# Edge weights multiplied into the low one-hot blocks by VectorE's comparison instead of by ScalarE, and source numbers split in floating point

## What is computed

```python
# GAT, twice (4 heads of 32)
h = (x @ W).reshape(N, H, C)
e = leaky_relu(alpha_s[src] + alpha_d[dst], 0.2)
e_exp = exp(e - segment_max(e, dst)[dst])
out = segment_sum(h[src] * (e_exp / segment_sum(e_exp, dst)[dst]), dst) + bias
...
# the layer behind them
feat_neigh = segment_sum(edge_val[:, None] * feat_in[edge_col], edge_row)
```

## Time and profile before

| | us |
|---|---|
| median of 3 runs | 12189.33 (12188.68 to 12192.55) |
| the profiled execution | 12168.16 |
| its span, first to last instruction | 12166.3 |
| first GAT pass, from the first gather to the last addition | 417 to 2829 |
| second GAT pass | 2953 to 5650 |

### The profile page before, as it was taken

The page is one execution under the profiler, slowest core; times in us unless marked ns, Lnnn a source line. Parts: engine busy times, 40 slices in busy tenths (PEclk is TensorE's granted clock), DMA queues, the critical chain, the costliest instruction groups (busy, mean ns, idle before and its releaser), DMA issues. The chain is left out here.

```text
span 12166.3 us, 91441 instructions
## 1 busy us (share of the span) xinstructions
PE 3704.8 (30%) x14114; PEld 2564.3 (21%) x14213; DVE 6446.5 (53%) x10684; ACT 2415.0 (20%) x6031; POOL 7481.0 (61%) x7840
## 2 busy tenths in 40 slices
PE   2212233332224555555200000003311111113987
PEld 2212222322113333333200000001211111112433
DVE  6445666664545665563655666665332222223877
ACT  1112333331212233221100000000000000001876
POOL 4676777774767766552576777772276777774023
PEclk7556666665557777778655555556655555556999
DMA  2255444443375665555247444442137333334866
GB/s 59 68 76 92 101 107 108 114 109 58 89 102 150 167 163 160 151 156 144 75 111 103 112 112 112 112 112 35 40 103 92 104 104 107 104 107 122 280 243 214
DMA packets 928552, 1422.94 MB, mean 117 GB/s; under 512 B 191108, under 2 KB 723306, under 8 KB 927992
## 3 DMA queue, kind: packets, MB, share of 16 engines
q0 software_dynamic: 277904, 662.94, 26.4%
q10 hardware_dynamic: 549664, 498.96, 14.4%
q1 hardware_dynamic: 100680, 257.93, 6.3%
HBM read 1064.18 MB, written 355.03 MB: 117 GB/s over the span
## 5 line engine op out<-in xcount | busy, mean ns | idle before, releaser
L818 POOL DMA_INDIRECT ring<-gat_table,index x3640 | 3470.8, 954 | 1536.9 <-issue 1054.2
L818 POOL DMA_INDIRECT ring<-b_table,index x1820 | 1730.2, 951 | 671.0 <-issue 526.0
L818 POOL DMA_INDIRECT ring<-kv_table,index x1820 | 1722.8, 947 | 594.6 <-issue 526.1
L961 PE MATMUL pairs<-hot_lo,hot_hi 128*128 128x128 f32 x6272 | 1173.9, 373 | 1845.9 <-PEq L959 1845.9
L961 PEld LDWEIGHTS pairs<-hot_lo,hot_hi 128*128 128x128 f32 x6272 | 1142.3, 286 | 1922.0 <-issue 1922.0
L993 ACT ACTIVATE hot_lo<-hot_lo,wt 128x128 f32<-128x128 f32 x3136 | 949.4, 387 | 1895.4 <-ACTq L991 1881.5
L1911 DVE TENSOR_TENSOR tb<-bt,att 128x1792 f32 x130 | 263.2, 2025 | 1661.7 <-DVEq L106 1661.7
L1143 DVE TENSOR_TENSOR first<-ring,first 128x924 f32<-128x924 f32 x260 | 292.5, 1125 | 1495.6 <-DVEq L106 1495.6
L1933 PE MATMUL bt<-ident,ring 128*128 128x128 f32 x1820 | 417.2, 421 | 1932.0 <-PEq L106 1932.0
L2066 ACT ACTIVATE r<-kept_ring,coef 128x448 f32<-128x448 f32 x1040 | 763.8, 758 | 184.9 <-ACTq L106 161.0
L713 PE MATMUL tp<-ident,stage 128*128 128x128 f32 x196 | 49.0, 427 | 2444.7 <-DVEq L700 2410.5
(11 more groups left out here) (414 smaller groups left out, 7926.4 us busy)
## 6 DMA issues: line engine op xcount, KB each, us to landing
kept_ring<-kept SPq DMA_DIRECT2D x260, 896.0 KB, 4.6
dense_weights<-dstage ACTq DMA_DIRECT2D x392, 512.0 KB
layer_out<-dense_weights ACTq DMA_DIRECT2D x98, 1568.0 KB, 14.8
kept<-tb ACTq DMA_DIRECT2D x132, 896.0 KB, 3.8
ring<-gat_table,index POOLq DMA_INDIRECT x3640
ring<-kv_table,index POOLq DMA_INDIRECT x1820
ring<-b_table,index POOLq DMA_INDIRECT x1820
col<-turned ACTq DMA_DIRECT2D x400, 32.0 KB
```

Source lines behind the costliest of these rows:

```text
L818: pool.indirect_dma_start(self.ring[:, r * UG + i, :], None, self.table, bass.IndirectOffsetOnAxis(self.index[:, half, at:at + 1], 0)).the ...
L961: mm = pe.matmul(self.ps[:, b, i * P:(i + 1) * P], self.hot_hi[:, u, 4 * b + i, :], self.hot_lo[:, u, 4 * b + i, :], start=False, stop=Fal ...
```

## The change

The constants and the preparation of columns change so that every column already carries the offset of its half: in `build_slots`, L470, the dummy value gets 8192 added for the lower partitions' half. The integers, the weights' copy and the semaphores `marked` go. VectorE divides the source number by 128 and rounds to a whole number by adding and subtracting 3 x 2^22, which gives the upper digit, and gets the lower one by subtraction. The low blocks are made one pair at a time by an instruction that compares the ramp with the lower digit and multiplies by the weight, both read as one value a partition. VectorE itself tells TensorE by `built`, after each quad, and frees the column only behind the phase's last block, since the weights are read from it. ScalarE keeps the fetch.

```diff
+WHOLE = float(3 << 22)
...
-                    c.go(dve.tensor_scalar(half[part, w, 0, part], ok[part, :], float(DUMMY), None, ALU.add))
+                    c.go(dve.tensor_scalar(half[part, w, 0, part], ok[part, :], float(DUMMY + q * PITCH), None, ALU.add))
...
-                c.go(dve.tensor_copy(self.wt[:, u, :], self.col[:, u, 1, part]))
-                c(dve.tensor_copy(self.num[:, 0, :], self.col[:, u, 0, part]))
-                dve.sem_inc(self.col_free[u], 1)
-                c(dve.tensor_single_scalar(self.num[:, 1, :], self.num[:, 0, :], 7, ALU.arith_shift_right))
-                c(dve.tensor_single_scalar(self.num[:, 0, :], self.num[:, 0, :], P - 1, ALU.bitwise_and))
-                c.go(dve.tensor_copy(self.lo[:, :], self.num[:, 0, :]))
-                c(dve.tensor_scalar(self.hi[:, :], self.num[:, 1, :], k.upper[:, 0:1], None, ALU.add))
-                c.reset()
+                source = self.col[:, u, 0, part]
+                c(dve.tensor_scalar(self.hi[:, :], source, 1.0 / P, 0.5 * (P - 1) / P, ALU.mult, ALU.subtract))
+                c(dve.tensor_scalar(self.hi[:, :], self.hi[:, :], WHOLE, WHOLE, ALU.add, ALU.subtract))
+                c(dve.scalar_tensor_tensor(self.lo[:, :], self.hi[:, :], float(-P), source, ALU.mult, ALU.add))
                 shape = [P, 4, P]
                 for b in range(QUADS):
                     four = slice(4 * b, 4 * b + 4)
-                    ramp = k.ramp[:, :].unsqueeze(1).broadcast_to(shape)
-                    dve.tensor_tensor(self.hot_hi[:, u, four, :], self.hi[:, four].unsqueeze(2).broadcast_to(shape),
-                                      ramp, ALU.is_equal)
-                    dve.tensor_tensor(self.hot_lo[:, u, four, :], self.lo[:, four].unsqueeze(2).broadcast_to(shape),
-                                      ramp, ALU.is_equal).then_inc(self.marked[b], 1)
+                    c.go(dve.tensor_tensor(self.hot_hi[:, u, four, :], self.hi[:, four].unsqueeze(2).broadcast_to(shape),
+                                           k.ramp[:, :].unsqueeze(1).broadcast_to(shape), ALU.is_equal))
+                    for i in range(4 * b, 4 * b + 4):
+                        w = at + i
+                        last = c.go(dve.tensor_scalar(self.hot_lo[:, u, i, :], k.ramp[:, :], self.lo[:, i:i + 1],
+                                                      self.col[:, u, 1, w:w + 1], ALU.is_equal, ALU.mult))
+                    c.until(last)
+                    dve.sem_inc(self.built[b], 1)
+                dve.sem_inc(self.col_free[u], 1)
+                c.reset()
...
-            for b in range(QUADS):
-                act.wait_ge(self.marked[b], 1)
-                act.sem_inc(self.marked[b], -1)
-                for j in range(4 * b, 4 * b + 4):
-                    last = act.activation(self.hot_lo[:, u, j, :], self.hot_lo[:, u, j, :], ACT.Copy,
-                                          scale=self.wt[:, u, j:j + 1])
-                last.then_inc(self.built[b], 1)
```

More of the change, by code:

```diff
@@ L890, in __init__ @@
         self.col = s.sb("col", [P, 2, 2, CH])
-        self.num = s.sb("num", [P, 2, PP], I32)
-        self.lo, self.hi, self.wt = s.sb("lo", [P, PP]), s.sb("hi", [P, PP]), s.sb("wt", [P, 2, PP])
+        self.lo, self.hi = s.sb("lo", [P, PP]), s.sb("hi", [P, PP])
         self.hot_hi, self.hot_lo = s.sb("hot_hi", [P, 2, PP, P]), s.sb("hot_lo", [P, 2, PP, P])
@@ L896, in __init__ @@
         self.ps = s.ps("pairs", [P, QUADS, 512])
-        self.marked, self.built, self.bank_free = ([k.sem(f"{x}{b}") for b in range(QUADS)] for x in (
-            "marked", "built", "bank_free"))
+        self.built, self.bank_free = ([k.sem(f"{x}{b}") for b in range(QUADS)] for x in ("built", "bank_free"))
         self.used = [k.sem(f"pairs_used{u}") for u in range(2)]
```

## The result

The kernel after took 11897.19 us (median of 4 runs, 11890.97 to 11906.11), the kernel before 12189.01 on the same chip: a ratio of 0.9762, interval 0.9745 to 0.9779. It is 292 us faster; the forecast was 11915. The profiled execution of after took 11906.11 us.

The account below looks back on a forecast made before the run. POOL's gathers bound long bands, ScalarE's late exponent the short ones. Pass two 245 plus pass one 40 less 10 for collisions gives 275: 12168 - 275 = 11893, and 21 more for the runs' median, 11915 us; range 11850 to 12090.

Parts of the forecast that it names:

- What bounds the kernel: POOL's gathers set the long bands; in short bands VectorE waits for ScalarE's late exponent, 698.3 us from 3525.
- the 325 put down as the most that POOL could give back: POOL's waits for ring space in two stretches of the passes, 27.2 and 297.8 us, as the gain's upper limit.
- The tile: Two-unit tile, second pass: quads 1.87 us, phase 8.7, exponent D + 20.5, multiply D + 21.3 (D its start), 35.7 in all.
- the 0.7 for stretched tensor_scalars: Two-unit tile: 0.7 us added for collisions, one tensor_scalar in nine as long as 522 ns against 341.
- Where the gain falls: Pass two from 3525 ends 245 us earlier, pass one from 1971 40 us; stages after 5650 are untouched.
- The 10 us for collisions: Both passes: more gathers beside blocks, up to 7 a phase instead of 5, at 10 to 80 ns each, cost 10 us.
- Rival 1: VectorE becomes the bound: quads near 2.3 us, tiles 39, pass two saves 150, pass one loses 30, 12070 us; chance 14%.
- Rival 2: Each of 7 gathers a phase waits x us longer: passes change -25+686x and -295+686x; 12320 at x=0.33; chance 7%.
- the 1.02 us in the earlier trace: POOL's DMA instruction beside seven two-operand tensor_scalars, against a median of 0.94: the 0.08 argued against rival 2.
- the stop as 0.15 us of cost: VectorE waits for each quad's last low block before marking it, counted as 0.15 us within the quad's 1.87.
- Rival 3: TensorE's clock might not rise with products spread along the builds: TensorE 42.5 us a tile, total 12130; chance 5%.
- Rival 4: The change does nothing because the exponent is late for another reason: 12189 us; chance 4%.

Follow-up runs that it names:

- Runs 1: Kernel before with only the floating-point split of the source numbers, ScalarE still multiplying by the weights: 12199.0 us, 1.0004 of before.
- run 2: Kernel before with the edge weights not multiplied in at all, so ScalarE's scaling pass is gone: 11867.87 us, 0.9729 of before.
- run 3: Kernel after with every low block computed twice, the second time into a tile nobody reads: 12369.51 us, 1.0145 of before.
- run 4: Kernel after without VectorE's stop behind the first three quads of a phase; the quad's last instruction marks it: 11976.55 us, 0.9821 of before.
- run 5: As run 4, with an added 160-column VectorE instruction between quads that reads ramp twice: 12108.92 us, 0.9957 of before.
- run 10: As run 4, with an added 128-column compare-and-multiply between quads that reads only ramp from SBUF besides scalar pointers: 12117.18 us, 0.9963 of before.
- run 6: As run 5, but the added instruction between quads has 40 columns instead of 160: 12045.45 us, 0.9904 of before.
- 7, two wide: Kernel after with a quad's low blocks made by two wide instructions, compare then multiply, stop kept: 11972.67 us, 0.9845 of before.
- 8, hi in PSUM: Kernel after with the tile hi (16 block numbers of a chunk) in PSUM instead of SBUF: 11863.43 us, 0.9751 of before.
- run 9: As run 4, without the stops between quads, but with the block numbers hi in PSUM: 11832.17 us, 0.9726 of before.
- 11, exponents first: Kernel after with ScalarE's exponents of a tile ahead of its first-phase stores and second-phase fetches and copies: 11942.67 us, 0.9816 of before.

## Why the prediction was right, point by point

*What bounds the kernel.* Right. Runs 1 and 2 separate the two halves of the change in the kernel before: the split does nothing, and taking ScalarE's pass away gives 325 us. That this is also the 325 put down as the most that POOL could give back is chance. In all attention gathers POOL's waits for ring space fell from 482.5 to 209.5 us in run 2 and to 213.8 in after; in after another 28 us were won behind the last gather of the passes (from 54.8 and 65.6 us to the pass's last finish down to 34.2 and 58.5), a term that the sentence on the 325 leaves out.

*The tile.* The 1.87 us of a quad, 8.7 of a phase (8.75), exponent at D + 20.5 (20.6), multiply at D + 21.3 (21.3) are as worked out. The compare-and-multiply form takes as long as the multiply-and-add that stood in the earlier trace rows; taking the same shape and operands as the nearest row was the right choice. The two-unit tiles came to 34.4 to 35.3 us, forecast 35.7: the 0.7 for stretched tensor_scalars was one term too many. Its 28 gathers alone take POOL 34.9 us (28 x (0.947 + 0.30)), so here the tile's length does not tell which of the two engines sets it; the waits of both are short.

*Where the gain falls.* Pass one ended 47.5 us earlier (2830.6 to 2783.1, forecast 40). Pass two, from its first gather to its last finish, took 251 less (forecast 245). At the next stage's first gather it is 297 in all (5998.2 to 5701.4), against 285 less 10. Two sums of the forecast don't come out of their terms: 3525 + 669 + 22 + 7 is 4223, not 4231, and 5650 less 5403 is 247, not 245. With them mended the forecast would have been some 10 us nearer. The 10 us for collisions did not come: the attention gathers were busy 3475.2 us, 3470.8 before. The profiled pair differs by 262 us only, since the stages behind, which the change doesn't touch, took 35 us longer in the profiled run of after. Gathers took 3 ns more there at the median, 0.947 us against 0.944 in the earlier trace rows; that is a third of it at most, and the rest is not explained. The medians differ by 292.

*Rival 1, VectorE the bound.* Not at this length of quad, but run 3 shows how near it was: with 1.03 us more a quad the short tiles get longer by all of it.

*Rival 2, the gathers held off.* For this kernel it did not happen, and the reason I gave, the 1.02 us in the earlier trace rows, was of the wrong kind. I looked for the hold beside the tensor_scalars. It sits at the wide comparison with two SBUF operands, which is in the kernel before as well; its gathers that begin in L937 or L939 were held 151 times, 29 us in all, and in after 115 times, 25 us. What decides is whether a held gather hands the next one into the next comparison. In after the next gather begins 0.90 + 0.30 = 1.20 us after the low blocks begin, and the next comparison 1.26 after (1.87 - 0.61), from a standstill: free, by 0.06 us (in after the first gathers that are held begin 0.05 into a comparison, so the room is some 0.1). In run 4 the comparison begins at 1.02 and runs to 1.63: caught. In run 3 the stop is kept and the next comparison begins 2.29 after the low blocks (1.87 + 1.03 - 0.61), while the second gather after a held one begins at 2.45: caught again, 428 times. So it is the lengths that decide, and the stop is only one of them. The prediction counted the stop as 0.15 us of cost; net of that cost it is worth 80 us, as long as hi lies in SBUF. I had not seen this. That the gathers came through was luck: the forecast was right with less room in the design than it seemed.

The rival's own sum holds where its condition was made true. In run 5 the gathers were busy 3745.1 us, 270 more than in after, which over 196 x 7 is x = 0.197; its formula gives -25 - 295 + 2 x 686 x 0.197 = -50 us against before, measured 12108.92 - 12164.86 = -56. In the same way run 10 gives -41, measured -48, run 6 -119 and -119, run 4 -196 and -216.

The runs side by side, held gathers counted as above at the wide comparison and the gap, busy us of all attention gathers from the row of each run:

| run | ratio | held | by, us | gathers busy | more than after |
|---|---|---|---|---|---|
| after | 0.9762 | 115 | 25 | 3475.2 | |
| 3, low blocks twice | 1.0145 | 428 | 167 | 3625.6 | 150 |
| 4, no stop | 0.9821 | 476 | 144 | 3599.5 | 124 |
| 6, gap of 40 | 0.9904 | 512 | 233 | 3676.4 | 201 |
| 5, gap of 160 | 0.9957 | 614 | 301 | 3745.1 | 270 |
| 10, gap, one operand | 0.9963 | 608 | 311 | 3754.4 | 279 |
| 7, two wide | 0.9845 | 740 | 140 | 3584.4 | 109 |
| 8, hi in PSUM | 0.9751 | 0 | 0 | 3456.3 | -19 |
| 9, and no stop | 0.9726 | 0 | 0 | 3453.9 | -21 |
| 11, exponents first | 0.9816 | 147 | 30 | 3476.6 | 1 |

The extra busy time is the held time less after's 25, within 10 us in each row.

*Rival 3, TensorE's clock.* It did not fall. In the tile shown the products of the second phase run at 1.00 although they wait for each quad; the mean clock from 3500 to 5370 is 0.79, 0.74 to 0.75 in the earlier trace rows for bands of that pass.

*Rival 4* is refuted by the result, and run 2 shows that it was ScalarE's pass that made the exponent late.

## What to carry to other kernels

To move work onto a busier engine can be free if it fills that engine's own waits; find from the trace where the wait is and how long, then test the cover by doubling the moved work. When GpSimd issues gathers, count the VectorE instructions with two SBUF operands beside them, and try one operand in PSUM (it must be measured: a copy with one SBUF operand held gathers too, see below). And a stop that looks like pure cost can keep two periodic engines from falling into step: after taking one out, or making a period longer, look at the other engine's mean duration, not only at the waits.

## What the hardware showed that I had not expected

A gather that begins while VectorE runs an instruction with two SBUF operands waits for its end and then takes 0.90 us: up to 1.45 us instead of 0.95 for a 512-column comparison, and 6.6 and 6.9 us beside the two 6272-column multiplies of a later stage, of two SBUF tiles each (the gathers of 8525.87 and 8539.02 in after). The first of them:

```profile
8524.93 6.69 DVE L1890 TENSOR_TENSOR fnt<-pads,at 128x6272 f32<-128x6272 f32 x1
8525.87 6.59 POOL L819 DMA_INDIRECT ring<-b_table,index  x1 [0.30 <-issue]
```

Beside the 924-column instructions with one operand in PSUM it takes 0.95. Beside trains of four tensor_scalars with pointers it is held by at most 0.13 us (run 4, 1.076 us); there it is rather the train that stretches, from 1.11 to 1.40 us in the longest rows of run 9. The Trainium skill, "SBUF — State Buffer", section "Who interferes with whom", states the half that decided here, that a VectorE instruction with two SBUF inputs contends with a GpSimd instruction that reads SBUF; these runs agree, with the hold of up to 0.5 us above. Its other half, on tensor_scalar in a 2-port mode, is the one I weighed in the prediction. The traces show no hold for a whole instruction beside these tensor_scalars, and whether they run in that mode no trace says.

Two SBUF operands are not the only thing that holds, so the theory as it stands ahead of run 10 is too narrow. A later stage of after has seven copies of 896 columns from SBUF to SBUF, 0.63 us each (L1896), which read one operand. Five gathers meet one; four are held, for up to 0.37 us, and the fifth began 0.01 before the copy and took 0.94. One of the four:

```profile
9459.17 0.63 DVE L1896 COPY att<-at 128x896 f32 x1 [0.71 <-DVE msq L1975]
9459.31 1.31 POOL L819 DMA_INDIRECT ring<-b_table,index  x1 [0.30 <-POOLq L107]
```

Queued behind a short instruction, such a comparison also shuts out a gather that began 0.08 us earlier (run 10); queued behind another comparison it does not (before). The Trainium skill says in the same section that whoever issues first gets the shared ports for the whole instruction; by that rule, with the begins taken from the profile, the gather of 4782.20 would have been free. The measurement decides.
